# Routing the tiles of a four-layer mixture of experts in five groups instead of six

## The reference

```
def _unipool_layer(xt, router, W1, W2):
    logits = xt @ router
    probs = softmax(logits);  w = max(probs);  idx = argmax(probs)
    for i in range(16):
        h = silu(xt @ W1[i]) @ W2[i]
        out += where(idx == i, w, 0)[:, None] * h
    return out
x = x + attention(xn) + scan(_unipool_layer over 4 routers, xn)
```

## Time and profile before

| quantity | value |
|---|---|
| three executions | 713.74, 713.78, 715.52 us |
| the profiled execution: its time | 715.52 us |
| the profiled execution: its span | 713.8 us |
| mean granted TensorE clock | 0.939 of full speed |

### The profile page before, as it was taken

One profiled execution on the slowest core, in us unless ns is written; L12 is line 12 of the kernel. 1 busy time (PEld: TensorE's weight loads), 2 busy tenths in 40 slices (PEclk: granted clock), 3 DMA queues, 4 the chain that ended last, 5 costly groups with the idle time before them and its releaser, 6 DMA issues.

```text
span 713.8 us, 15342 instructions
## 1 busy us (share of the span) xinstructions
PE 615.8 (86%) x5063; PEld 526.9 (74%) x5063; DVE 470.3 (66%) x1357; ACT 442.4 (62%) x1120; POOL 384.6 (54%) x433
## 2 busy tenths in 40 slices
PE   2969999969999699986999959888798799989996
PEld 2659999929998299883899735775587578768885
DVE  7443346753468524684321188979979999998856
ACT  3364466635656356571666758896957788785643
POOL 6353024450244403444254531368779999998974
PEclk9989999989999799995999979987989999999999
DMA  9964242126221262212122120000000000000002
GB/s 181 299 239 96 51 122 68 48 60 133 67 60 44 68 130 67 57 37 64 31 73 66 36 60 2 1 1 1 2 1 1 1 1 1 1 1 1 2 2 60
DMA packets 61950, 39.91 MB, mean 56 GB/s; under 512 B 9298, under 2 KB 57458, under 8 KB 61874
## 3 DMA queue, kind: packets, MB, share of 16 engines
q1 hardware_dynamic: 57394, 29.64, 17.6%
q0 software_dynamic: 4480, 9.30, 3.9%
HBM read 20.32 MB, written 18.59 MB: 55 GB/s over the span
## 4 chain that ended last, share of the span: by engine, by line
PE 56%; DVE 25%; ACT 8%; issue 4%; another core or an unknown queue 3%; POOL 3%; DVEq 0%; ACTq 0%; POOLq 0%
PE PS L2181 16%; PE PS L2166 15%; DVE W2s L1301 3%; PE PS L2085 2%; PE PS L2398 2%; ACT W1s L1826 2%; PE PS L2119 2%; PE PS L2157 2%; PE PS L2346 2%; DVE W1s L1446 2%; DVE W1s L1415 1%; PE PS L2508 1%; DVE PS L1439 1%; DVE PS L1417 1%
## 5 line engine op out<-in xcount | busy, mean ns | idle before, releaser
L711 POOL DMA_INDIRECT sorted_x<-xrow,pos x93 | 90.5, 973 | 176.2 <-DVE pos L1138 114.3
L2181 PE MATMUL PS<-W2s,hbuf 128*128 x992 | 140.1, 284 | 5.4 <-ACT hbuf L1644 5.4
L2166 PE MATMUL PS<-xTs,swt 128*128 128x128 f32 x992 | 131.5, 276 | 6.2 <-ACT xTs L1639 5.7
L2181 PEld LDWEIGHTS PS<-W2s,hbuf 128*128 128x128 f32 x992 | 126.7, 191 | 6.4 <-issue 6.3
L2166 PEld LDWEIGHTS PS<-xTs,swt 128*128 128x128 f32 x992 | 121.0, 192 | 8.0 <-DVE swt L1190 4.0
L1644 ACT ACTIVATE hbuf<-PS 128x512 f32<-128x512 f32 x124 | 73.8, 596 | 42.5 <-PE PS L2166 34.8
L1190 DVE COPY swt<-W1s 128x512 f32 x84 | 36.9, 441 | 90.5 <-PE PS L2166 73.0
L1651 ACT ACTIVATE xrow<-PS,hbuf 128x144 f32<-128x144 f32 (+1 forms) x124 | 46.8, 377 | 54.5 <-PE PS L2181 49.7
L2398 PE MATMUL PS<-ident,W1s 128*128 128x128 f32 x512 | 66.0, 285 | 4.5 <-POOL W1s L827 4.5
L2398 PEld LDWEIGHTS PS<-ident,W1s 128*128 128x128 f32 x512 | 62.6, 200 | 5.7 <-POOL W1s L827 4.9
L1826 ACT ACTIVATE W1s<-W1s,ab 128x128 f32<-128x128 f32 x168 | 51.3, 391 | 15.9 <-DVE W1s L1449 15.9
(11 more groups left out here) (395 smaller groups left out, 1382.9 us busy)
## 6 DMA issues: line engine op xcount, KB each, us to landing
hbuf<-sorted_x SPq DMA_DIRECT2D x124, 65.0 KB
sorted_x<-slotbuf SPq DMA_DIRECT2D x45, 130.0 KB, 3.2
W2s<-in_L_ffn_W_dram SPq DMA_DIRECT2D x16, 256.0 KB
W1s<-in_L_ffn_W_dram SPq DMA_DIRECT2D x1, 4096.0 KB
sorted_x<-slotbuf SPq DMA_DIRECT2D x1, 2015.0 KB, 14.5
sorted_x<-xrow,pos POOLq DMA_INDIRECT x109
xres<-in_L_attn_x_dram SPq DMA_DIRECT2D x4, 256.0 KB, 3.6
xrow<-results SPq DMA_DIRECT2D x4, 256.0 KB, 4.1
```

The costliest lines, as they stand in the source:

```text
L711: pool.indirect_dma_start(xs_dram[l + 1][:, :], bass.IndirectOffsetOnAxis(ap=pos[:, t:t + 1], axis=0), xrow[:, t % NR, 0:XW], None).then_i ...
L2166: m = pe.matmul(PS[:, 2 + n, f * P:(f + 1) * P], w1st[:, (c - 1) % WB, f * P:(f + 1) * P], xTs[:, n, :], start=True, stop=True)
L2181: m = pe.matmul(PS[:, 4 + n, 0:w], hTs[:, n, f * P:(f + 1) * P], W2s[:, f * YW:f * YW + (E - 1) * NF + w][:, bass.ds(w2, w)], start=(f == ...
```

## The change

The four groups from tile 16 on (4, 4, 4 and 3 tiles) become three: tiles 16 to 22 are one group, 23 to 26 the next, and 27 to 30 the last. The places of the steps in the loop follow, and the third entry of `PACE` goes, so that from group 2 on a scatter waits for `pos_ready` alone.

```
-    GROUPS = ((0, 8), (8, 16), (16, 20), (20, 24), (24, 28), (28, NS))
+    GROUPS = ((0, 8), (8, 16), (16, 23), (23, 27), (27, NS))
     NGR = len(GROUPS)
-    PACE = (10, 10, 11)
+    PACE = (10, 10)
...
-    CHOOSE_AT = {12: 0, 20: 1, 24: 2, 27: 3}
-    WEIGH_AT = {13: 0, 21: 1, 25: 2, 28: 3}
-    ROOMS_AT = {14: 0, 22: 1, 26: 2, 29: 3}
-    PLACE_AT = {15: 0, 23: 1, 27: 2, 30: 3}
-    TANH_AT = {10: 0, 18: 1, 22: 2, 26: 3, 30: 4}
-    RANKS_AT = {11: 0, 19: 1, 24: 2, 27: 3, 31: 4}
+    CHOOSE_AT = {12: 0, 20: 1, 26: 2}
+    WEIGH_AT = {13: 0, 21: 1, 27: 2}
+    ROOMS_AT = {14: 0, 22: 1, 28: 2}
+    PLACE_AT = {15: 0, 23: 1, 29: 2}
+    TANH_AT = {10: 0, 18: 1, 25: 2, 29: 3}
+    RANKS_AT = {11: 0, 19: 1, 26: 2, 30: 3}
```

## The result

The changed kernel took 723.88 us (median of four, 720.76 to 727.78), the kernel before 714.65 (median of four, 713.74 to 716.24): ratio 1.0144, 95% interval 1.0095 to 1.0194. It is slower, and by more than the forecast's whole range allowed. The profiled execution took 723.82 us for a span of 722.0, against 713.8 before; clock 0.936 against 0.939.

A forecast was written before the change was run, and what follows sets the result against it. The routing chain, DVE and PE in turns, was taken to bound the gap between layers. A saving of 1.9 and a burst price of 2.1 gave +0.2 us a layer, +0.6 over three: 714.4 us, range 713 to 715.7.

The forecast's parts named there:

- the price of the unpaced run of scatters: Six scatters running unpaced before PE's last tile in a routed layer's loop: one late delivery and more, 2.1 us a layer.
- the forecast saving of 1.9 us: Routed layers, one group fewer: last choice 2.1 us earlier, less 0.2 us for a four-tile last group; -1.9 us a layer.
- The upper end of my bounds: Burst in the loop: PE's tiles lose 1.8 us, group 3's ranks reach DVE 2.2 us late; 4.0 us a layer.
- late through the burst: Ranks of group 3 and last tiles each reach DVE 2.4 to 2.8 us late; 717.7 us middle, 720 upper; chance 0.27.
- The saving of the missing group: End of a routed layer's loop: the last group's choice comes at 141.85 instead of 143.94 us, 2.1 us a layer.
- Scatters 16 to 22: POOL, routed layer: seven scatters in a row from about 134.4 us, 1.27 us apart, held only by `pos_ready`.
- test (2): Transposes 28 to 30: one gap of 3.3 us or more; late rival: two or more, or group 3's rooms idle over 2 us.
- POOL's end: Layer's end: four last scatters instead of three, last start 1.2 us later; taken as costing nothing, at most +1.0 us a layer.
- the cover of 3.7 us: Layer's end: 3.7 us from loads beginning to PE's first tile without a wait, slack that may cover the 1.2 us.
- The clock: Gap between layers: PE stands for less time, granted clock stays up, saving up to 1 us a layer; 711.4 us, chance 0.05.
- the rival of the full saving: Loop of the routed layers: the burst costs little, so -5.7 us in all, 708.1 us; chance 0.28.

The follow-up runs named there:

- the paced groups: Changed kernel's five groups with PACE = (10, 10, 11), so scatters 16 to 19 wait again for result tiles 27 to 30: 711.15 us, ratio 0.9919 to the kernel before.
- a plain one in a run of 7.4 us: Changed kernel with two plain DMAs a tile for each indirect scatter, placing by row numbers left out: 682.13 us on chip C, 680.27 us on chip E.

## Why the prediction was wrong

- **The failed step is the price of the unpaced run of scatters.** I took 2.1 us a layer, "one late delivery and a small part of a second". Measured, the last tile comes 12.00 - 5.85 = 6.15 us late, to 0.05 us in all six layers of the two profiles with the delay. Layers 1 and 2 became 3.5 and 3.6 us longer; with the forecast saving of 1.9 us this makes the price 5.4 to 5.5 us (4.6 and 4.9 on chip D). The upper end of my bounds, 4.0, was too low too. Three deliveries to ACT and one to DVE are late, and not by one amount: the lateness grows through the run, 1.7, 4.3 and 6.2 us, and ACT, which works in order, can pass the last tiles on only behind the latest of them (143.77). The rows had runs of three and four scatters and one late delivery each. I read them as a price for each burst; it grows with the hand-overs from PE that fall into the burst.
- **The rival "late through the burst" was right** in place (ranks of group 3 and the last tiles), sign and mark: rooms of group 3 idle for 4.60 us, last choice at 147.58 us where I had set 145 as its bound. Its size was too small: 717.7 in the middle, 720 at most, against 723.88. I had given it 0.27, less than the forecast's 0.36.
- **The saving of the missing group was right.** Forecast: last choice 2.1 us earlier. From the transpose of tile 30 to the last choice: 7.93 us before, 6.05 on chip E, 5.95 with the paced groups on chip A: 1.9 to 2.0 us.
- **Scatters 16 to 22** started at 133.78 and ran 1.27 us apart: as predicted (134.4). No gap stands in transposes 28 to 30 (1.98, 1.98 us): my test (2) looked for the gap one tile too early, and only its other sign, the idle rooms of group 3, showed.
- **POOL's end.** The last scatter starts 4.1 us after the last `pos` as worked out (3 x 1.27 + 0.3). PE stood 0.36 us for the loads before the next layer (164.31 in the timeline above), so the cover of 3.7 us was used up. With punctual completions POOL becomes the bound (2.32 us idle for the DMA on chip E). From the last scatter's start to the next layer it took 4.36 us at the least in any layer of the changed kernel's three profiles and of the paced one's; the paced groups stood at this bound in two of three layers (4.38 and 4.36), which is a likely reason that they gain 0.8% and not more.
- **The sum.** Layers 1 and 2 lose 3.5 and 3.6 us; the third gains 2.4, and there the clock differs: from 325 to 337 us the granted clock was 0.50 before, and 0.50, 0.87 and 0.98 in three equal parts of 325 to 337 us after. Together the layers make 4.7 of the 8.2 us of span. In the other profile of the kernel before, on chip D, the third layer took 89.56 us and not 91.86, so 2.3 us of that gain are a matter of the execution. The rest of the 8.2 us stands in code that the change does not touch: 0.4 us in the fourth layer, and from its last transpose to the end it took 312.7 us before and 316.0 after, but 310.8 in the changed kernel's second profile, and 316.3 and 316.6 in others. So these 3.3 us are a matter of the execution, not of the change. Without the two the change costs the routed layers about 4.7 + 2.3 = 7 us, an estimate that fits chip D, where the two profiles differ by 6.8 us there (2.65, 3.03 and 1.15). The windows over the same work late in the second block, before and after, show one place where they differ (columns: stretch, its length, busy time of PE, weight loads, DVE, ACT, POOL, granted clock, DMA):

```profile
685.00:688.00 3.00, 3.00 (x48) 2.64 (x47) 0.98 (x6) 0.28 (x1) 2.72 (x4) 1.00 0.00 0
```

```profile
690.00:693.00 3.00, 3.00 (x40) 2.61 (x40) 0.48 (x3) 0.99 (x1) 2.84 (x3) 0.70 0.03 5
```

- **The clock.** PE was busy for about half of the time between the late deliveries, and its granted clock fell: 1.00 in the first of the windows below, 0.66 in the second, and 0.50, the lower level (1.2 GHz), in the third. The last tile's second matmuls took 2.29 us instead of 1.15, which is 1.1 of the 6.15 us of lag. The earlier trace rows had 0.75 behind this point; I had counted the clock only as a possible gain.

```profile
137.00:141.00 4.00, 2.01 (x24) 1.73 (x23) 1.38 (x6) 0.81 (x4) 3.09 (x4) 1.00 0.15 50
141.00:145.00 4.00, 1.91 (x9) 1.57 (x10) 0.90 (x5) 1.62 (x4) 1.06 (x2) 0.66 0.10 33
145.00:149.00 4.00, 4.00 (x11) 2.86 (x12) 3.30 (x20) 1.88 (x4) 1.87 (x2) 0.50 0.05 17
```

The rule that compute and DMA cannot slow each other (the Trainium skill, "SBUF — State Buffer", section "SBUF: two separate sides") would have given 708.1 us. By the times it fits chip E, where the change gains 1.2%, and not the first result, nor the late completions on chips A, B and D. The traffic is the same in all of them, and plain DMAs of the same rows left PE alone on chip B, so what was late there is not shown to be a matter of SBUF's ports.

What stays open: by what path an indirect DMA holds up PE's completions; whether a plain one in a run of 7.4 us would do it on a chip that has the delay (both runs of that kernel fell on chips without it; three indirect ones in a row last 3.5 us and did it on chip D, seven plain ones last 3.7 us and did not on chip B); what makes the chips differ, and whether a chip keeps its kind, since each was seen once; and whether the recording of signals for the profile has a part in the delay, which no run was made to test. On chip E the gain was 8.2 us where the rival of the full saving had 5.7; no profile of the kernel before was taken there, so the rest is not placed.

## What to carry to other kernels

On some chips a run of three or more indirect DMAs of GpSimd without a pause made what PE finished known late, and the lateness grew with the hand-overs from PE that fell into the run. In a kernel like this one, keep the scatters paced while another engine waits for PE, or put 0.7 us of other work behind every second one (on chip C, where nothing was late, the kernel with these pauses was 0.8% slower than the kernel before). But held-back scatters collect at the end of the layer and then bound the loads; start them earlier (smaller first groups) rather than faster. And compare kernels only on the same chip, and on more than one: here the same change was 1.4% slower in the first result, 1.2% slower on chip D and 1.2% faster on chip E.

## What the runs showed of the hardware

- The kernel before took 713 to 716 us on three chips and 697 to 699 on two, 2.1 to 2.8% apart. Kernels with runs of scatters have gaps of up to 4.7 us in the loop on the former, and no gap over 2.5 us after tile 3 of the routed layers on the latter.
- While PE's completions reached ACT up to 6.2 us late, PE started 0.14 us after the end of the ACT copy that it waited for (137.98 to 138.12).
- An indirect DMA of 128 rows keeps POOL for 1.27 us, issue included, a plain one for 0.53 us. With the plain ones, which leave out the placing, the changed kernel took 4.2% less than the kernel before.
- The tables of semaphore updates differ in the same way. An indirect or plain DMA of POOL counts its semaphore 16 times as it lands. For the 124 scatters of its four layers the changed kernel's trace holds about half of these 1984 updates on chip D (984) and all of them on chip E; with plain DMAs on chip B, all 1488 of the three routed layers are there, and about half of those of the fourth layer's indirect ones. Updates are missing where completions are late; which causes which is not shown.
